# Two layers of gated attention and feed-forward on one core: passes joined at their boundaries, transposed rows stored once

## What is computed

```python
x = x + tanh(gx[0]) * (attn0(layernorm(x), fside, routers) @ Wo + bo)      # 16 heads, softmax over 512 keys
x = x + tanh(g[0])  * bit_linear(silu(conv3(bit_linear(layernorm(x), w1))), w2)
x = x + tanh(gx[1]) * (attn1(layernorm(x), ctx) @ Wo1.T + bo1)             # 16 heads, 77 keys
# recurrence over the 8 batches, all 512 rows side by side, c starts at in_c:
for xt in layernorm(x):
    f, i = sigmoid(xt @ wf.T + c @ uf.T + bf), sigmoid(xt @ wi.T + c @ ui.T + bi)
    c = f * c + i * tanh(xt @ wc.T + c @ uc.T + bc)
x = x + tanh(g[1]) * tanh(layernorm(x) @ wo.T + c_final @ uo.T + bo2)
```

## Time and profile before

| what | value |
|---|---|
| median of 3 runs | 2726.01 us (2723.91 to 2733.47) |
| profiled execution, its own time | 2719.8 us |
| its span | 2718.0 us |
| mean granted TensorE clock | 0.944 |
| busy PE / DVE / ACT / POOL | 2356.2 / 1419.5 / 1028.4 / 599.7 us (87 / 52 / 38 / 22%) |
| bytes moved | 182.56 MB, mean 67 GB/s |
| attention, feed-forward | first transfers at 120 and 1039.8 |
| context attention, recurrence, output | first transfers at 1612.9, 2029.0 and 2604.3 |

### The profile page before, as it was taken

One profiled execution on the slowest core, in us unless ns is written; L12 is line 12 of the kernel. 1 busy time (PEld: TensorE's weight loads), 2 busy tenths in 40 slices (PEclk: granted clock), 3 DMA queues, 4 the chain that ended last, 5 costly groups with the idle time before them and its releaser, 6 DMA issues. The chain is left out here.

```text
span 2718.0 us, 40799 instructions
## 1 busy us (share of the span) xinstructions
PE 2356.2 (87%) x16348; PEld 1549.0 (57%) x16348; DVE 1419.5 (52%) x1733; ACT 1028.4 (38%) x1185; POOL 599.7 (22%) x204
## 2 busy tenths in 40 slices
PE   7259999999999984799999857999968999999978
PEld 6235555555555542445444325666646888888756
DVE  4345565565565543567777647787745222222124
ACT  3324454454444441355555533444423111111111
POOL 0004654545554562000000002232320000000000
PEclk9679999999999986999999978999988999999989
DMA  7701011011010004111111021122224111111166
GB/s 239 181 33 38 16 46 41 11 44 31 24 45 10 14 13 132 32 48 58 51 46 47 17 86 53 67 83 70 68 93 144 42 44 44 45 44 48 45 234 261
DMA packets 104571, 182.56 MB, mean 67 GB/s; under 512 B 17252, under 2 KB 39780, under 8 KB 99358
## 3 DMA queue, kind: packets, MB, share of 16 engines
q1 hardware_dynamic: 100110, 172.84, 19.2%
q10 hardware_dynamic: 4368, 8.39, 0.8%
HBM read 122.07 MB, written 59.15 MB: 67 GB/s over the span
## 5 line engine op out<-in xcount | busy, mean ns | idle before, releaser
L976 DVE TENSOR_REDUCE att_mx<-att_sn 128x2 f32<-128x1024 f32 x256 | 313.6, 1225 | 169.1 <-PE att_sn L821 166.3
L733 POOL TENSOR_TENSOR att_es<-att_es,att_num 128x2048 f32<-128x2048 f32 x64 | 292.7, 4574 | 15.6 <-ACT att_num L904 9.3
L904 ACT ACTIVATE att_num<-att_st 128x2048 f32<-128x2048 f32 x128 | 240.6, 1879 | 141.0 <-PE att_st L809 81.0
L729 POOL TENSOR_TENSOR att_es<-att_num 128x2048 f32<-128x2048 f32 x32 | 145.9, 4559 | 370.7 <-PE att_pj L791 340.8
L2290 ACT ACTIVATE rec_ga<-rec_g,rec_bg 128x512 f32<-128x512 f32 x84 | 57.2, 689 | 312.0 <-PE rec_g L2189 312.0
L821 PE MATMUL att_sn<-att_kh,att_qh 32*128 32x512 f32 x512 | 127.6, 494 | 29.3 <-DVE att_mx L976 29.3
L1533 DVE TENSOR_TENSOR ffn_hs<-ffn_h,ffn_fb 128x1024 f32<-128x1024 f32 x64 | 78.0, 1219 | 115.9 <-PE ffn_h L1233 106.8
L1233 PE MATMUL ffn_h<-ffn_xqt,ffn_w 128*128 128x512 bf16 x512 | 125.1, 389 | 13.1 <-DVE ffn_hs L1533 13.1
L821 PEld LDWEIGHTS att_sn<-att_kh,att_qh 32*128 32x128 f32 x512 | 48.4, 185 | 148.2 <-DVE att_mx L976 110.9
L1840 POOL TENSOR_TENSOR xat_pr<-xat_e,xat_rd 128x1232 f32<-128x1232 f32 x32 | 73.1, 2283 | 241.8 <-DVE xat_rd L2026 235.0
L784 PE MATMUL att_pj<-att_num,att_v 128*32 128x512 f32 x1024 | 123.5, 601 | 1.0 <-issue 1.0
(11 more groups left out here) (375 smaller groups left out, 5859.6 us busy)
## 6 DMA issues: line engine op xcount, KB each, us to landing
att_x<-in_x SPq DMA_DIRECT2D x8, 1024.0 KB, 5.4
att_f<-in_fside_BxSxS SPq DMA_DIRECT2D x8, 1024.0 KB, 7.7
heads<-att_o SPq DMA_DIRECT2D x32, 256.0 KB
ffn_ol<-heads SPq DMA_DIRECT2D x8, 1024.0 KB, 5.3
ffn_x<-in_x SPq DMA_DIRECT2D x8, 1024.0 KB, 5.4
x<-ffn_xr SPq DMA_DIRECT2D x32, 256.0 KB, 2.0
xat_x<-x SPq DMA_DIRECT2D x8, 1024.0 KB, 5.2
xat_xr<-x SPq DMA_DIRECT2D x8, 1024.0 KB
```

The source lines that it names most:

```text
L729: pool.tensor_tensor(ES[:], E[0][:], E[1][:], ALU.add).then_inc(s_sum, 1)
L733: pool.tensor_tensor(ES[:], ES[:], E[k][:], ALU.add).then_inc(s_sum, 1)
L904: act.activation(E[k][:], st_ps[:], ACT.Exp, scale=SCALE).then_inc(s_exp, 1)
L976: dve.tensor_reduce(MX[c % 2][:, m // 2, 2 * DH * (m % 2):2 * DH * (m % 2) + DH + 1:DH], sn_ps[:], AX, ALU.max, negate=True).then_inc(s_ma ...
```

## The change

The change joins the passes by work that is moved over their boundaries; the barrier itself stays. Which matmuls are done, and on what, is the same but for the first rows' place and the way of the transposed rows.

1. **Tiles kept.** `rows` (x), `weights_a` and `weights_b` (high and low), `rows_b`, the row weights of the recurrence and a `Lead` of small tiles (pick, bias, gates, undo, taps, conv bias, quantised rows and their factors) are allocated in `build` and handed from pass to pass.
2. **Attention** loads the small tiles early, ACT copies the bias and takes two tanh, DVE makes the bias's low half. In its last turn it loads Wo, x(0), heads(0) and splits them (`following`), runs `first_rows(t)` inside the last step, and DVE normalises and quantises those rows in `late`.
3. **Feed-forward** starts at the transposes; of the loads W1, W2 and heads(1) are left. In its tail it loads x2(0), Wq and Wo of context attention, takes moments, normalises, splits.
4. **Context attention** starts with its weights and first rows ready. In its last two turns ACT loads wf, wi, wc through one staging tile and copies, DVE subtracts; then moments and normalisation of x3(0).
5. **Recurrence** starts with those; it loads the u-side weights only. ACT copies each transposed block from PSUM to `xw` and from there to the high half; DVE makes the low half from `xw`; `xw`, one float32 copy, is stored in `columns`. The last batch isn't stored.
6. **Output** runs batch 7 first from the tiles that the recurrence left, loads `columns` (1 MB a batch), splits on ACT and DVE, and finishes the last batch in four pieces.

The diff, cut to its core:

```diff
+    LAST_STEP = HEAD + AV + [("out", 0), ("s", 1), ("out", 1), ("s", 2)] + SUM + [("out", 2), ("s", 3), ("out", 3)] + TAIL
...
+            sp.wait_ge(made["f"], QUADS)
+            sp.dma_start(F[:], kxn(lead.Wo)).then_inc(s_nextw, 16)
+            sp.wait_ge(made["x"], QUADS)
+            sp.dma_start(X[:], rows(x, 0)).then_inc(s_nextx, 16)
+            sp.wait_ge(made["k"], QUADS)
+            sp.wait_ge(s_store, C * 16)
+            sp.dma_start(f32(W_QO[1][1][:]), rows(o_s, 0)).then_inc(s_nexto, 16)
             turn(B - 1)
...
+            def first_rows(t):
+
+                if t == 0:
+                    pe.wait_ge(s_ones, 8)
+                    pe.wait_ge(s_bolo, 1)
+                    pe.wait_ge(s_nextlo, 2)
+                    pe.wait_ge(s_max, QUADS * N_MAX)
+                if t >= 2:
+                    pe.wait_ge(s_xadd, t - 1)
...
+                pe.matmul(out, lead.pick[:], lead.BO[:], start=True, stop=False)
+                for k in range(C):
+                    pe.matmul(out, W_QO[1][0][:, k, own], W_QO[0][0][:, k, :], start=False, stop=False)
+                    pe.matmul(out, W_QO[1][0][:, k, own], W_QO[0][1][:, k, :], start=False, stop=False)
+                    last = pe.matmul(out, W_QO[1][1][:, k, own], W_QO[0][0][:, k, :], start=False, stop=(k == C - 1))
+                last.then_inc(s_x1, 1)
...
             def late():
+                ln.aggregate(dve, rows0)
                 for task in LATE:
                     job(task)
...
+                dve.wait_ge(ln.s_rstd, B + 1)
+                for t in range(T):
+                    rows0.inc(dve.tensor_scalar(F[:, t, :], X[:, t, :], ln.mv[:, t, 0:1], ln.rstd[:, t:t + 1],
+                                                ALU.subtract, ALU.mult))
+                lead.row_maxima(dve, F, rows0)
+                dve.wait_ge(s_undo, 16)
+                lead.quantised_rows(dve, F, rows0)
...
+            def following(i):
+
+                if i == 1:
+                    dve.wait_ge(s_nexthi, 1)
+                    dve.tensor_tensor(W_QO[0][1][:], F[:], f32(W_QO[0][0][:]), ALU.subtract).then_inc(s_nextlo, 1)
+                if i == 2:
+                    dve.wait_ge(s_nexthi, 2)
+                    dve.tensor_tensor(W_QO[1][1][:], f32(W_QO[1][1][:]), f32(W_QO[1][0][:]),
+                                      ALU.subtract).then_inc(s_nextlo, 1)
```

Feed-forward (its tail on DVE), context attention (DVE after a group) and recurrence (ACT):

```diff
+            dve.wait_ge(s_nextx, 16)
+            ln.moments(dve, after)
             for group in range(GROUPS):
                 rounded(B - 1, group)
-            for t in range(T):
+            ln.scale(dve, B, after)
+            for i, weights in enumerate((WO, O)):
+                out_rows(B - 1, i, False)
+                dve.wait_ge(s_nexthi, i + 1)
+                dve.tensor_tensor(weights[1][:], raw[i], f32(weights[0][:]), ALU.subtract).then_inc(s_nextlo, 1)
+            for t in range(2, T):
                 out_rows(B - 1, t, False)
...
+                at = (b - B + 2) * C + c if isinstance(b, int) else -1
+                if 0 <= at < 6 and at % 2:
+                    next_low(at // 2)
+                if isinstance(b, int) and b == B - 1:
+                    if c == 2:
+                        dve.wait_ge(s_nextx, 16)
+                        ln.moments(dve, Steps(s_next, 0, ln.DVE_N))
+                    if c == 3:
...
+                        ln.scale(dve, B, after)
...
                 for c in range(C):
                     act.wait_ge(s_pj, a * C + c + 1)
-                    act.activation(XT[0][:, c, :], pj_ps[c % 2][:], ACT.Copy).then_inc(s_hi, 1)
...
+                    act.activation(XW[:, c, :], pj_ps[c % 2][:], ACT.Copy).then_inc(s_xw, 1)
+                    act.wait_ge(s_xw, a * C + c + 1)
+                    act.activation(XT[0][:, c, :], XW[:, c, :], ACT.Copy).then_inc(s_hi, 1)
```

557 lines of the change are left out of this document (326 added, 231 removed).

## The result

The changed kernel takes 2682.43 us, median of 4 runs (2677.83 to 2685.18), and the kernel before 2725.11, median of 4 (2723.91 to 2733.47): a ratio of 0.983, 95% interval 0.981 to 0.985. That is faster by 43 us or 1.7%, where 55 us and 2671 were predicted. The profiled execution took 2680.6 us against 2719.8: 39.2 less.

What follows compares the result with a forecast made beforehand. PE bounds the kernel inside passes, so gains lie at four boundaries and the end: -12.7 - 21.9 - 2.6 - 10.4 - 7.7 = -55.3 us, 2664.5 profiled, 2671 against the median; forecast 2660 to 2681 (0.62), range 2650 to 2694.

Steps and rivals of the forecast that it cites:

- slots aren't idle: Rival for the whole kernel: added jobs cost their full price, -40 us in all, 2686 us; chance 0.14.
- Attention, start: Start of attention: three activations and the bias subtract delay the score maxima and PE's next step, +3.4 us.
- Attention, last turn: Splits of Wo and heads(0) ahead of steps (7,1) and (7,2): 3.2 and 0.3 us, bounds 0 and 8.4.
- First rows: Attention's last step: two of four first rows stand ahead of POOL's last additions, +4.2 us; the others cost nothing.
- Attention's end and feed-forward's start: Normalising and quantising four row tiles adds 8.0 us to attention's tail; feed-forward's hidden group follows 22.0 after its start.
- Boundary 1: Attention to feed-forward: PE's hidden group behind the first hs at 1078.8 instead of 1091.52, -12.7 us, bounds -20 and -5.
- Feed-forward to context attention: Loads, splits and normalisation move into feed-forward's tail; ACT's first column block comes earlier, -21.9 us, bounds -19 and -23.
- Row weights: Context attention's last two turns: splits of wf, wi, wc, statistics and normalisation cost +9.5 of 12 us, bounds 5 and 13.
- Recurrence: Starts with rows and weights ready, gates 12.1 us earlier; steady turns cost 0, with 1 us a turn kept in range.
- Boundary 3: Context attention to recurrence, row-weight cost and earlier gates together: -2.6 us, bounds -8 and +3.
- Output: Output pass: PE starts without a load, -9.4 us, and loses less to a slow clock, -1; together -10.4.
- The signs: Feed-forward near 1057 and 1079; context attention's first block within 6 us, gates within 9; recurrent ACT waits at most 0.5.

Runs made afterwards that it cites:

- run 5: Changed kernel with the bias copy, two tanh and the bias's low-half subtract ahead of the normalisation in attention: 2676.5 us.
- run 1: Changed kernel without the splits of Wo and heads(0) in attention's last turn: 2671.9 us.
- runs 3 and 4: Changed kernel with heads(1) loaded ahead of W2, 2680.2 us; then also with DVE's low half of heads(1) behind the first hs, 2666.8 us.
- Run 10: Changed kernel with two staging tiles, row-weight copies and subtracts inside groups where their engine waits for PE, and statistics behind the last group: 2663.2 us.
- run 7: Changed kernel with each transposed column block of the recurrence copied once more by ACT, into a spare tile: 2679.7 us.

## Why the prediction was right, and where it was not

Faster was right, and the time was 11 us off. 2682 is inside the range of 2650 to 2694, but 1 us outside the 2660 to 2681 that the forecast itself was to hold: it lies where the range reaches into "slots aren't idle".

- **Attention, start.** +3.4 predicted. The first maximum came at 202.84 behind `bolo` (203.6 in the prediction, in a pass that stood 0.7 later), and the local length grew by 2.9. Moved (run 5), it costs nothing.
- **Attention, last turn.** This step failed: "I count 3.2 of the 4.2 ... so I take 0.3", 3.5 for the pairs, bounds 0 and 8.4. They cost 11.9, beyond the upper bound; 12.0 by run 1 on the same stretch (10.0 to the fourth chain, since the first rows behind them gave 2.0 back). The first pair cost 4.6 for 3.2, the second 7.3 for 0.3. That ACT would be ahead at (7,2) was right; that DVE would be in a wait there was not, and the row with 1.88 was no evidence for that place. The other parts that the sum lacked are in the rows above: 2.7 of waiting for POOL's additions and 7.2 of slower matmuls. The sentence on the ports, +1.5 by its rule, pointed the right way at the right instruction and had no part in the sum.
- **First rows.** +4.2 taken, +2.3 measured and +4.3 in run 1. This stretch is 18.2 to 18.5 us in seven of the kernels with first rows and 20.3 in the other five, all seven at a granted clock of 1.00 and all five at 0.86, so the size that was forecast is one of two outcomes. Beyond that the other two, costed at nothing under POOL's chain, gave 1.6 back. That stretch ran at a granted clock of 0.76 before, with PE idle for 9.7 of it, and at 1.00 now, with 3.9 idle.
- **Attention's end and feed-forward's start.** The tail was 7.93 for 8.0 and the start of the transfers 1061.7 for 1056.8, late by the pairs. From there 22.1 for 22.0. Part of that is luck: 5 MB at 2.6 make 13, and the prediction doesn't derive the landing at 16.4 that it takes. ACT starts on heads(1) at 16.6. The order of the work holds, and runs 3 and 4 show each of its pieces: the queue, then DVE. Boundary 1 as a whole is -7.7 where -12.7 was forecast, and all of that is the pairs' overrun, less what the first rows gave back.
- **Inside feed-forward** the prediction took nothing. 2.9 us were lost there; the last section shows a group that makes 2.7 of it.
- **Feed-forward to context attention.** -21.9, to the tenth, statistics in the old tail included. 3.2 of it were given back in the first 70 us of context attention, which the prediction hadn't.
- **Row weights.** This step failed too: "All of it adds 6.9 + 3.1 + 2 = 12. I take +9.5 and keep 5 and 13". With 1.8 in the pass's end it was 15.4, beyond the upper bound of 13. The reasoning "what it does late PE soon feels" was right in kind, but the term was made of DVE's durations alone; the loss was 10.4 of PE's waits, with DVE itself waiting 7.2 for ACT at one of the three subtracts, and 5.0 of slower matmuls. Run 10 shows a better reason to doubt it: the same work costs 2.1 where DVE waits for PE anyway.
- **Recurrence.** Start -12.7 for -12.1, turns 0.3 for 0. Boundary 3 is then +2.8 instead of -2.6, by the row weights alone.
- **Output.** -9.5 for -9.4. The first 4 us now ran 17 matmuls at a clock of 1.00 (9 at 0.50 before), and 384 of them took 2.2 less. The Trainium skill (TensorE: Matmul & The Clock Gate, What's actually happening) says that activity releases a throttled default. With 1.9 us of idle ahead instead of 11.4 the trace agrees here, its 89.56 for 91.75. At the starts of feed-forward and context attention the gain that I had worked out from that rule didn't come: the 20 us from the second hidden group ran at 0.90, and the 25 us from the first block on ACT at 0.79, where they ran at 0.91 and 0.83 before. The recurrence's first 20 us from its first gate ran at 0.87 for 0.86.
- **End.** 5.7 us behind PE for 5.0: -7.0.
- **The signs.** Those of context attention's first block (4.99), the gates (7.25) and the output pass held. Feed-forward's two moments came 5 late. "No wait of over 0.5 on ACT in a recurrent turn" can't be used as it is worded: ACT waits 1.95 for a transposed block in the turn of run 7; the wait that was meant is the 0.34.

Of the rivals, "slots aren't idle" (2686) was the nearest in kind and overstated in the recurrence. By the terms, the removed work gave what was forecast, 1 us more even, and two added jobs took back 14 us more than forecast, both beyond their own bounds. The mechanism of what was removed was right; that the whole stayed inside the range in spite of the two is owed to its width. The drifts in feed-forward and context attention took 6 more. That is more than the 16 that the profiled execution misses by (2680.6 against 2664.5), the rest being what the first rows, the attention start, recurrence start and output did better.

What stays open: the overall time of the kernels run once, which carry 2 to 6 us of drift in places that their edit doesn't touch; why the clock falls at one phase of a turn and not at another; and whether a second staging tile without the new places, or the new places without the tile, would have done for the row weights.

## What to carry over

A job moved into an earlier pass is as cheap as the place in the other engine's wait that it finds: look per group for the stretch where that engine idles on the bottleneck, and give the load time and, where two loads would share one, a buffer of its own. Where it can't be placed so, its duration is too low a price: here 4.6 us of subtracts on DVE cost 11.9, and 11.9 us of work on DVE cost 15.4, by the waits of PE that they made and slower matmuls beside them. Check what GpSimd does beside it. Judge such an edit by a length between two near events, since marks 90 us apart drifted by 3.0 where the effect was 2.9.

## What the runs showed of the hardware

- A DVE subtract of two SBUF tiles beside POOL's additions takes longer, by about what is left of the addition in progress: in the rows below POOL's first addition (4.6 of the 11.08) ends near 997.6, and the subtract 2.1 behind that. The same 128x2048 subtract took 4.99 us in the changed kernel and 3.91 and 3.12 in runs 3 and 4, by its start against POOL's, and 2.28 free. In those two POOL's pair of additions took 11.1 instead of 9.21: it paid for the subtract in turn. The kernel heads_before_w2:

```profile
993.04 11.08 POOL L766 TENSOR_TENSOR att_es<-att_es,att_num 128x2048 f32<-128x2048 f32 x2
...
995.83 3.91 DVE L1135 TENSOR_TENSOR weights_b_l<-weights_b_l,weights_b_h 128x2048 fp32r<-128x2048 f32 x1
```

- The granted clock behind the same wait isn't always the same. One group of 96 small matmuls in feed-forward, with 2.90 us of idle ahead of it in both kernels, took 6.09 in the changed kernel and 3.40 in the kernel before. The changed kernel:

```profile
1535.88 6.09 PE L1373 MATMUL ffn_c<-ffn_hs,ffn_dg 32*32 32x512 f32 x96 [2.90 <-ACT ffn_ss L1503]
```

The kernel before:

```profile
1543.44 3.40 PE L1246 MATMUL ffn_c<-ffn_hs,ffn_dg 32*32 32x512 f32 x96 [2.90 <-ACT ffn_ss L1385]
```

The granted clock was 0.51 in the first and 1.00 in the second. PE's work and wait just ahead are the same; what differs is the moment, and that in the changed kernel the load of x2(0), issued at 1532.43, moves 192 GB/s in that wait where 2 GB/s moved before. The load alone doesn't decide it: all twelve kernels with it have the same 2.90 of idle there, and the group takes 3.50 in tail_no_splits, at a clock of 1.00, and 4.75 to 6.09 in the others. Whether it has a part is open. Such a group is worth up to 2.7 us, as much as many of the terms here, and the prediction's reading of the order of the work didn't foresee it.
